# Copying the full attention's scores out of PSUM with VectorE, and giving the freed bank to the other attentions

## The reference, cut to what matters

```python
scores = softmax(einsum('bhqd,bhkd->bhqk', q, k) * scale)
entropy = -sum(scores * log(clip(scores, 1e-8)), axis=-1)
max_attn = scores.max(axis=-1)
influence = scores.sum(axis=-2)
importance = -entropy.mean(1)*0.4 + max_attn.mean(1)*0.3 + influence.mean(1)*0.3
_, idx = top_k(importance, 51)
```

## Time and profile before

| what | value |
|---|---|
| median of 3 runs | 1926.42 us (1925.96 to 1930.85) |
| the profiled execution | 1930.84 us, of it 1928.7 us from first to last instruction |
| mean granted TensorE clock | 0.692 of full speed |
| busy: PE, DVE, ACT, POOL | 1487.1, 1223.3, 1001.2, 389.4 us |
| first and last score matmul of the full attention | 229.5 and 1778.7 us |
| one batch's period in the middle of the run | 211.6 us for 64 slots |

### The profile page before, as it was taken

How to read it: one execution, slowest core, us unless ns; L and a number is a source line. 1 busy time by engine, 2 the same in 40 slices (tenths; PEclk the granted TensorE clock), 3 DMA queues, 4 the chain that set the end, 5 groups by cost and what they waited for, 6 DMA issues and landing times.

```text
span 1928.7 us, 25028 instructions
## 1 busy us (share of the span) xinstructions
PE 1487.1 (77%) x7949; PEld 652.0 (34%) x7949; DVE 1223.3 (63%) x3203; ACT 1001.2 (52%) x2478; POOL 389.4 (20%) x900
## 2 busy tenths in 40 slices
PE   1786797888788788788788878878878878678645
PEld 1333432343334333344234333334334322321312
DVE  1503556877787477856787478857786577787211
ACT  1051376457556555656556655565654657546122
POOL 3102301330133012310233023301221012110100
PEclk9566577659666777677766876677766867665555
DMA  2110210122012110122012111211011002200100
GB/s 59 31 47 11 57 34 17 42 50 41 6 50 52 23 23 14 45 46 45 14 39 52 28 19 36 53 26 33 14 34 36 12 14 45 27 13 12 17 8 5
DMA packets 65619, 59.17 MB, mean 31 GB/s; under 512 B 11936, under 2 KB 63184, under 8 KB 65488
## 3 DMA queue, kind: packets, MB, share of 16 engines
q1 hardware_dynamic: 65488, 57.58, 14.2%
HBM read 39.10 MB, written 18.27 MB: 30 GB/s over the span
## 4 chain that ended last, share of the span: by engine, by line
PE 50%; DVE 22%; ACT 15%; issue 7%; POOL 3%; DMA 2%; SPq 0%; ACTq 0%; POOLq 0%; DVEq 0%
PE bank L1276 8%; PE bank L1316 7%; DVE junk L978 5%; ACT setup L827 4%; PE bank L1268 4%; PE bank L1244 3%; PE bank L1221 3%; PE bank L1299 3%; DVE nm L946 3%; ACT pT L813 2%; DVE nmB L1068 2%; DVE nm L933 2%; PE bank L1259 2%; PE bank L1251 2%; PE bank L1200 2%
## 5 line engine op out<-in xcount | busy, mean ns | idle before, releaser
L827 ACT ACTIVATE setup<-bank,nmB 128x512 f32<-128x512 f32 x512 | 350.4, 684 | 340.7 <-DVE nmB L1068 339.5
L978 DVE SCALAR_TENSOR_TENSOR junk<-bank,thr,setup 128x512 f32<-128x512 f32 x512 | 379.2, 741 | 96.5 <-POOL thr L695 92.6
L1068 DVE TENSOR_REDUCE nmB<-bank 128x1 f32<-128x512 f32 x512 | 351.1, 686 | 111.5 <-PE bank L1268 111.3
L1268 PE MATMUL bank<-k_stacks,q_stacks 48*128 48x512 bf16 x512 | 254.5, 499 | 151.8 <-DVE junk L978 150.1
L695 POOL TENSOR_TENSOR thr<-lnZ,nmB 128x1 f32<-128x1 f32 x512 | 96.7, 190 | 1223.5 <-ACT lnZ L830 1223.2
L813 ACT ACTIVATE pT<-bank 128x512 f32<-128x512 f32 x320 | 174.3, 590 | 133.5 <-PE bank L1229 132.1
L1276 PE MATMUL bank<-setup,rz 128*1 128x512 f32 x1024 | 203.0, 879 | 0.0
L1268 PEld LDWEIGHTS bank<-k_stacks,q_stacks 48*128 48x128 bf16 x512 | 49.9, 98 | 384.2 <-DVE junk L978 285.3
L1221 PE MATMUL bank<-q_stacks,k_stacks 55*128 55x384 bf16 (+3 forms) x512 | 138.9, 346 | 36.6 <-ACT pT L813 30.7
L933 DVE TENSOR_REDUCE nm<-bank 128x4 f32<-128x512 f32 x128 | 86.5, 687 | 65.8 <-PE bank L1196 65.8
L909 ACT ACTIVATE p<-bank 115x512 f32<-115x512 f32 x128 | 75.1, 587 | 81.9 <-PE bank L1435 81.8
(11 more groups left out here) (195 smaller groups left out, 2327.9 us busy)
## 6 DMA issues: line engine op xcount, KB each, us to landing
part_dram<-part SPq DMA_DIRECT2D x16, 768.0 KB, 3.2
q_stacks<-part_dram SPq DMA_DIRECT2D x192, 64.0 KB
k_stacks<-part_dram SPq DMA_DIRECT2D x192, 64.0 KB
s_stacks<-part_dram SPq DMA_DIRECT2D x48, 128.0 KB
x<-in_L_attn_a_x_dram SPq DMA_DIRECT2D x8, 256.0 KB, 7.2
x_dram<-x SPq DMA_DIRECT2D x8, 256.0 KB, 2.2
x<-x_dram SPq DMA_DIRECT2D x8, 256.0 KB, 2.9
out_dram<-x SPq DMA_DIRECT2D x8, 256.0 KB, 2.2
```

The costliest lines, as they stand in the source:

```text
L827: act.activation(E[:, n % NE, :], RING[n % RN][:, :], ACT.Exp, bias=nmB[mb % 2][:, h, t:t + 1], accum_out=Z[mb % 2][:, h, t:t + 1]).then_i ...
L978: dve.scalar_tensor_tensor(out=junk[:, :], in0=RING[n % RN][:, :], scalar=thr[mb % 2][:, h, t:t + 1], in1=E[:, n % NE, :], op0=ALU.max, op ...
L1068: dve.tensor_reduce(nmB[mb % 2][:, h, t:t + 1], RING[n % RN][:, :], AX_X, ALU.max, negate=True).then_inc(s_bm, 1)
L1268: pe.matmul(RING[n % RN][:, :], qst[1][0:B_SC, h, t * P:(t + 1) * P], kst[1][0:B_SC, h, :], start=True, stop=True).then_inc(s_bs, 1)
```

## The change

- DVE no longer only takes the maximum of a tile of scores. One `tensor_scalar` multiplies the tile by -1, writes it to an SBUF buffer `negs` (four of them), and gives its row minimum, which is the negated maximum.
- ACT's exponential reads `negs` with scale -1; DVE's entropy step reads `negs` too, with signs turned (`min` for `max`), and POOL's subtraction is turned round.
- PE's ring has two banks (0 and 1) and is free when the copy has been made. `LEAD` is 2: PE writes tile n at the head of its slot n-2.
- The entropy step comes one slot later (`STT_LAG = 2`): tile n at the end of DVE's slot n+2.
- Bank 2 goes to the causal and the small attention: their first tiles and minus-max tiles take banks 3, 4 and 2 in turn.

```diff
+        NS = 4
+        negs = [sb(f"negs{i}", [P, T]) for i in range(NS)]
...
-        RING = (bank[0], bank[1], bank[2])
+        RING = (bank[0], bank[1])
+        TILE_BANK = (3, 4, 2)
...
-        LEAD = 1
+        LEAD = 2
+        STT_LAG = 2
...
-                use(3 + u % 2, z + A1_AT + u // 2, "a1", b, u)
+                use(TILE_BANK[u % 3], z + A1_AT + u // 2, "a1", b, u)
...
-                        act.activation(E[:, n % NE, :], RING[n % RN][:, :], ACT.Exp, bias=nmB[mb % 2][:, h, t:t + 1],
+                        act.activation(E[:, n % NE, :], negs[n % NS][:, :], ACT.Exp, scale=-1.0,
+                                       bias=nmB[mb % 2][:, h, t:t + 1],
...
-                    dve.scalar_tensor_tensor(out=junk[:, :], in0=RING[n % RN][:, :], scalar=thr[mb % 2][:, h, t:t + 1],
-                                             in1=E[:, n % NE, :], op0=ALU.max, op1=ALU.mult,
+                    dve.scalar_tensor_tensor(out=junk[:, :], in0=negs[n % NS][:, :], scalar=thr[mb % 2][:, h, t:t + 1],
+                                             in1=E[:, n % NE, :], op0=ALU.min, op1=ALU.mult,
...
-                        dve.tensor_reduce(nmB[mb % 2][:, h, t:t + 1], RING[n % RN][:, :], AX_X, ALU.max, negate=True
-                                          ).then_inc(s_bm, 1)
+                        if n >= NS:
+                            dve.wait_ge(s_be, n - NS + 1)
+
+                        dve.tensor_scalar(negs[n % NS][:, :], RING[n % RN][:, :], -1.0, None, ALU.mult, ALU.min,
+                                          accum_out=nmB[mb % 2][:, h, t:t + 1]).then_inc(s_bm, 1)
...
-                    if before:
-                        entropy(*before)
+                    lagging = main_tile(g - STT_LAG)
+                    if lagging:
+                        entropy(*lagging)
...
                     if n >= RN:
-                        pe.wait_ge(s_bn, n - RN + 1)
+                        pe.wait_ge(s_bm, n - RN + 1)
```

More of the change, by code:

```diff
@@ L197, in hybrid_block @@
         s_rows = sem("constant_rows_in_stacks")
-        s_full = {k: sem(f"bank{k}_uses_written") for k in (3, 4, 7)}
-        s_free = {k: sem(f"bank{k}_uses_read") for k in (3, 4, 5, 7)}
+        s_full = {k: sem(f"bank{k}_uses_written") for k in (2, 3, 4, 7)}
+        s_free = {k: sem(f"bank{k}_uses_read") for k in (2, 3, 4, 5, 7)}
         s_xin = sem("x_loaded")
@@ L256, in hybrid_block @@
         s_bs = sem("full_scores")
-        s_bm = sem("full_maxima")
+        s_bm = sem("full_scores_copied_with_maxima")
         s_be = sem("full_exponentials")
@@ L536, in hybrid_block @@
             for h in range(H):
[L537 removed]
+                use(TILE_BANK[h % 3], z + S1_AT + h // 2, "s1", b, h)
                 use(5, z + S2_AT + S_GANG * (h // HPQ) + h % HPQ, "s2", b, h)
@@ L549, in hybrid_block @@
                 use(7, z + DOWN[k], "down", k, b)
-        turn = {3: {}, 4: {}, 5: {}, 7: {}}
+        turn = {2: {}, 3: {}, 4: {}, 5: {}, 7: {}}
         for slot, k, name in sorted(uses, key=lambda e: e[0]):
@@ L603, in _ @@
                             if b:
-                                last = ("a2", b - 1, N2 // 2 * (f + 1) - 1)
-                                sp.wait_ge(s_full[4], turn[4][last] + 1)
+                                u = N2 // 2 * (f + 1) - 1
+                                k = TILE_BANK[u % 3]
+                                sp.wait_ge(s_full[k], turn[k]["a2", b - 1, u] + 1)
                             load_half(0, b, f, AL)
@@ L694, in _ @@
                         pool.wait_ge(s_bz, n + 1)
-                        pool.tensor_tensor(thr[mb % 2][:, h, t:t + 1], lnZ[mb % 2][:, h, t:t + 1],
-                                           nmB[mb % 2][:, h, t:t + 1], ALU.subtract).then_inc(s_bt, 1)
+                        pool.tensor_tensor(thr[mb % 2][:, h, t:t + 1], nmB[mb % 2][:, h, t:t + 1],
+                                           lnZ[mb % 2][:, h, t:t + 1], ALU.subtract).then_inc(s_bt, 1)
                     for b, a in own_slots(g):
@@ L811, in _ @@
                                     act.wait_ge(s_pv[0], 3 * (NG * b + gang - 1) + c + 1)
-                                act.wait_ge(s_full[3 + u % 2], turn[3 + u % 2]["a2", b, u] + 1)
+                                act.wait_ge(s_full[TILE_BANK[u % 3]], turn[TILE_BANK[u % 3]]["a2", b, u] + 1)
                                 act.activation(pT[:, js[0]:js[0] + len(js), c * T:c * T + WIDTH[c]],
-                                               bank[3 + u % 2][:, :].rearrange("p (j q) -> p j q", j=len(js)),
-                                               ACT.Exp).then_inc(s_free[3 + u % 2], 1)
+                                               bank[TILE_BANK[u % 3]][:, :].rearrange("p (j q) -> p j q", j=len(js)),
+                                               ACT.Exp).then_inc(s_free[TILE_BANK[u % 3]], 1)
                         for j in range(NG):
@@ L928, in causal_maxima @@
                 def causal_maxima(b, u):
-                    k, blocks = 3 + u % 2, FIRST_TILES[u % NF]
+                    k, blocks = TILE_BANK[u % 3], FIRST_TILES[u % NF]
                     h = 2 * (u // NF) + blocks[0][0]
@@ L943, in small_maxima @@
                 def small_maxima(b, h):
-                    k = 3 + h % 2
+                    k = TILE_BANK[h % 3]
                     dve.wait_ge(s_full[k], turn[k]["s1", b, h] + 1)
@@ L987, in own_importance @@
                     dve.wait_ge(s_imp, 4 * b + 1)
-                    dve.scalar_tensor_tensor(out=t2[:, :, :], in0=t1[:, :, :], scalar=LOG_CLIP, in1=thr[s][:, :, :],
+                    dve.scalar_tensor_tensor(out=t2[:, :, :], in0=t1[:, :, :], scalar=-LOG_CLIP, in1=thr[s][:, :, :],
                                              op0=ALU.add, op1=ALU.subtract).then_inc(s_imp, 1)
                     dve.wait_ge(s_imp, 4 * b + 2)
-                    dve.scalar_tensor_tensor(out=t3[:, :, :], in0=t2[:, :, :], scalar=0.4 / 0.3, in1=rz[s][:, :, :],
+                    dve.scalar_tensor_tensor(out=t3[:, :, :], in0=t2[:, :, :], scalar=-0.4 / 0.3, in1=rz[s][:, :, :],
                                              op0=ALU.mult, op1=ALU.add).then_inc(s_imp, 1)
@@ L1074, in _ @@
                         if a == A_TMAX - 1:
-                            dve.wait_ge(s_free[3], turn[3]["a1", b, N1 - 2] + 1)
-                            dve.wait_ge(s_free[4], turn[4]["a1", b, N1 - 1] + 1)
+                            for u in range(N1 - 3, N1):
+                                k = TILE_BANK[u % 3]
+                                dve.wait_ge(s_free[k], turn[k]["a1", b, u] + 1)
                             dve.tensor_tensor(nm[0][:, 1:NT, :], nm[0][:, 1:NT, :], nml[:, 1:NT, :], ALU.min
@@ L1181, in causal_scores @@
                 def causal_scores(b, u):
-                    k = 3 + u % 2
+                    k = TILE_BANK[u % 3]
                     claim(k, "a1", b, u)
@@ L1235, in weigh @@
                     g, c = w // 3, w % 3
-                    for u in (g * G2 + CHUNK_END[c] - 1, g * G2 + CHUNK_END[c]):
-                        pe.wait_ge(s_free[3 + u % 2], turn[3 + u % 2]["a2", b, u] + 1)
+                    for u in range(g * G2 + max(0, CHUNK_END[c] - 2), g * G2 + CHUNK_END[c] + 1):
+                        pe.wait_ge(s_free[TILE_BANK[u % 3]], turn[TILE_BANK[u % 3]]["a2", b, u] + 1)
                     if c == 0:
@@ L1427, in _ @@
                             claim(5, "tmax", b)
-                            pe.wait_ge(s_free[4], turn[4]["s1", b, H - 1] + 1)
+                            k = TILE_BANK[(H - 1) % 3]
+                            pe.wait_ge(s_free[k], turn[k]["s1", b, H - 1] + 1)
                             transpose_max(1, bank[5]).then_inc(s_mt, 1)
```

3 lines of the change are left out of this document (1 added, 2 removed).

## The result

The changed kernel takes 1999.76 us (median of 4 runs, 1994.43 to 2006.28) against 1928.63 for the kernel before in the same session (4 runs, 1925.96 to 1941.84). The ratio is 1.0347, 95% interval 1.0314 to 1.038: slower, by about 71 us, where the forecast was 42 more. The profiled execution took 2001.17 us, its span 1999.0.

What follows compares the result with a forecast made beforehand. No engine was full; PE and DVE went nearly in step, a slot costing about the longer one's work. Terms summed to +5.8 us a period, times 7.3 = +42 us on 1926.4: 1968 us, range 1895 to 2010.

Steps and rivals of the forecast that it cites:

- The release of the ring: PE's score-matmul head is released one DVE instruction later, by the copy: +7.5 us a period, bounds 2.7 to 9.5.
- 11 chains: Of PE's 14 head waits a period, 11 counted as separate slot chains, each paying the copy's 0.68 us.
- The copy for the maximum: DVE's copy with accumulator, 751 ns against 686 for the maximum: +1.4 us a period, between 0 and 4.2.
- The entropy step out of SBUF: DVE's entropy step with two SBUF inputs, 695 to 752 ns against today's 741: no change, 0.
- The rival of half rate: DVE's entropy step with two SBUF sources at half throughput, 1.28 us: about 2095 us in all; chance 0.03.
- DVE against GpSimd: Two-input entropy step contends with POOL: +1.5 us a period, between 0 and 4.4; rival with +4.4, 1989 us, chance 0.04.
- The exponential: ACT's exponential out of SBUF goes from 684 to some 724 ns, hidden by ACT's idle time: 0.
- The lag of the entropy step: Entropy step one slot later removes DVE's 10.5 us of threshold waits: -0.9 us a period, up to 4.
- Three tile banks: A third bank for first tiles shortens PE's waits for DVE and ACT: -3.7 us a period, from 0 to -8.
- the mechanism's own range: Whole-kernel time if the forecast's mechanism holds: 1940 to 2005 us, chance 0.63.
- PE's clock: PE's granted clock, 0.73 in the period, taken as unchanged; nothing in the sum follows it if it moves.
- The rival in which DVE gets ahead: DVE finishes whole slots early in PE's long slots, so the release costs nothing: about 1880 us; chance 0.20.

Runs made afterwards that it cites:

- before_gate: Kernel before with one added wait: the score matmul of tile n also waits for the maximum of tile n-1; 2011.98 us, ratio 1.0449.
- copy_only: Kernel before with the SBUF copy read by exponential and entropy step; ring of three, lead, lag and tile banks as before; 1972.1 us, 1.025.
- copy_act: Kernel before with the SBUF copy used by the exponential alone, the entropy step still reading PSUM; 1954.52 us, ratio 1.0126.
- stt_lag1: Changed kernel with the entropy step back at one slot's lag (STT_LAG 1 for 2); 2003.22 us, ratio 1.0361.
- lead1_lag1: Changed kernel with LEAD 1 for 2 and the entropy step at one slot's lag; 1913.29 us, ratio 0.9868.
- lead1: Changed kernel with LEAD 1 for 2, so PE's head waits for the copy of tile g-1; 1904.45 us, ratio 0.9878.
- ring3_lead1: Changed kernel with three ring banks, two banks for first tiles, and LEAD 1; 1910.83 us, ratio 0.9882.
- rz_lag: Changed kernel with DVE's inversion of the sums and the influence matmuls one slot later; 1993.09 us, ratio 1.0323.
- ring3: Changed kernel with bank 2 given back: three ring banks, two for first tiles, LEAD still 2; 1926.54 us, ratio 0.9997.
- copy_gate: Kernel before with the SBUF copy for exponential and entropy step, plus the added wait for the maximum of tile n-1; 2023.91 us, 1.0453.

## Why the prediction was right, step by step

**The release of the ring** is what makes the change slow, as forecast. It is shown from both sides: put in alone it costs 4.5%, taken out of the changed kernel (by LEAD, which also moves the score matmuls, or by the ring, which also takes the third tile bank away) it gives 3.4 to 4.5%. The term was 7.5 us a period. Alone, in before_gate, it is 6.9 in a middle period, but 66.7 us from the first score matmul to the last instead of 7.3 x 7.5 = 55: there the multiplication by 7.3 falls short, since the first and last batches pay more than a middle one. (For the whole change it holds: 7.3 x 10.45 = 76, measured 70.3.) Its wait is also a little dearer than the copy's: at the boundary at 999.64 us of before_gate the head starts 0.84 us after the maximum has started, where it started 0.75 after the copy. In the changed kernel the heads' waits grew by 11.7 a period (14 waits, now 18) and 79.2 over the run. 18 x 0.68 = 12.2 agrees with that better than my 11 chains: I had not counted the heads that came just in time before and wait now.

**The copy for the maximum**, +1.4, measures 0: 684 ns for 686. The nearest row by form (751) was the wrong one. The bound by size and source (684, the product out of PSUM in the earlier trace rows) was the price.

**The entropy step out of SBUF**, 0, was right: median 743, within 695 to 752. The rival of half rate, about 1.28 us, is refuted. The Trainium skill has this rule in the Vector Engine (DVE) Microarchitecture Reference, section "Points that are easy to get wrong"; the measured median, 743 ns, decides against it for this instruction.

**DVE against GpSimd**, +1.5 a period or 11 us, was too small: copy_only less copy_act is 24 us, near the bound of 4.4 a period that the rival took (32 us). But a sum per period was the wrong place for it: the middle periods of the two kernels are equal, and what contention costs shows in the first and last batches. I had priced only DVE's delay. The timeline of the kernel after shows both sides:

```profile
1059.68 2.18 POOL L678 TENSOR_TENSOR rest<-qf,part 128x512 f32<-128x512 f32 x1
...
1060.78 1.64 DVE L985 SCALAR_TENSOR_TENSOR junk<-negs,thr,setup 128x512 f32<-128x512 f32 x1
...
1062.04 0.42 POOL L701 TENSOR_TENSOR thr<-nmB,lnZ 128x1 f32<-128x1 f32 x1 [0.18 <-ACT lnZ L837]
...
1062.42 1.15 POOL L678 TENSOR_TENSOR rest<-qf,part 128x512 f32<-128x512 f32 x1
...
1062.96 1.16 DVE L985 SCALAR_TENSOR_TENSOR junk<-negs,thr,setup 128x512 f32<-128x512 f32 x1
...
1063.09 0.60 PE L1280 MATMUL bank<-k_stacks,q_stacks 48*128 48x512 bf16 x1 [2.13 <-DVE negs L1078]
```

The entropy step of 1060.78 takes 1.64 us beside POOL's 2.18, the next 1.16 beside POOL's 1.15, the threshold 0.42 instead of 0.19, and PE's head at 1063.09 had waited 2.13 us. The mean threshold went from 190 to 286 ns and the layer norm, on whose result PE's transposes wait, from 794 to 935. That a DVE instruction with two SBUF inputs contends with a GpSimd instruction that reads SBUF is in the Trainium skill, SBUF — State Buffer, section "Who interferes with whom"; the trace agrees (1.64 us beside POOL, for a median of 743 ns).

**The exponential**, 0, is 718 ns where some 724 was said. Whether it is free is open: copy_act has nothing else new than this and the copy, and it is 1.3% slower; of the 22.2 us between the spans 5.8 lie ahead of the first score matmul (235.3 for 229.5), where the two kernels are the same.

**The lag of the entropy step**, -0.9, measures 0 (stt_lag1, lead1_lag1). "What is late next" was answered wrongly: not the inputs of DVE's maxima, but the inversion of the sums, which the change left at slot g-1.

**Three tile banks**, -3.7 a period or -27 us. The waits in front of the first tiles did fall in the changed kernel: for DVE's maxima from 39.4 us to 9.3, for ACT from 30.7 to 24.9. Of the first the small attention's are 15.3 in the kernel before, 4.6 in before_gate and 1.1 in the changed kernel:

```profile
L1310 PE MATMUL bank<-kcst,s_stacks 48*128 48x115 bf16 x512 | 54.9, 253 | 16.5 <-DVE nm L946 15.3
```

```profile
L1311 PE MATMUL bank<-kcst,s_stacks 48*128 48x115 bf16 x512 | 54.0, 252 | 5.8 <-DVE nm L946 4.6
```

So in before_gate, with two tile banks, they fall too (in all to 22.1 for DVE and 21.2 for ACT): when PE is held at its head, the tiles' banks are free by the time it comes. So 17 of the 30 us are the other term seen again. Between lead1 and ring3_lead1 the bank is worth 20 us of waits, about 2.7 a period, and no time that could be separated from the other difference between them.

**The sum.** Every term was added; the costs do not add (2.5% and 4.5% make 4.5%). Heads and tile banks are two doors to the same queue: time lost at one is not lost at the other. A release too small outside the middle, too small a contention, and gains of lag and tile bank that mostly weren't there, left the forecast at +5.8 a period for +10.45. Of the 10.45 before_gate alone shows 6.9; which part of the change makes the other 3.5 no run says. The time still lies in the mechanism's own range of 1940 to 2005, near its upper end. The direction and the main term were right for the reason given. Without the terms that measured nothing or nearly nothing (+1.4, -0.9, -3.7) the same sum would have given +9.0 a period, 66 us, near the 71 measured; but part of that nearness is luck, since the 1.5 for contention in it is not found in a middle period and the release is larger at the ends of the run than in the middle.

**PE's clock** was set down as unchanged, with the remark that nothing in the sum followed it. It wasn't: 25.7 of the 70.3 us are PE's busy time. The rival in which DVE gets ahead did not come: waits at the heads rose. What it asked for came with LEAD = 1.

**Open.** What makes PE's busy time move. Over all these kernels the same 7949 matmuls take from 1429.4 us (lead1_lag1) to 1529.6 (copy_only), and more idle time doesn't mean a longer run: lead1 has 33.5 us more of it than before and is 20.9 us shorter. The idle share of the span doesn't order the clocks either: 23% goes with 0.676 (copy_act) and 0.692 (before), 24 to 25% with 0.669 (after) and 0.695 (lead1). No run was made that changes the clock alone. The nearest is the start of before and before_gate, where the same instructions at 0.74 and 0.51 of full speed bring the first score matmul at 229.5 and 241.6 us: there a lower clock goes with a later time and nothing in the program differs, but it is one pair of executions. For the rest of the run, whether the clock is a cause or a sign is not settled; nor is which of the copy and the longer exponential costs copy_act its 1.3%.

## What to carry to other kernels

Ask of a ring which instruction in the reader's in-order queue frees the bank at the moment when the writer wants it. More lead with fewer banks can move that instruction later, though each reader frees its bank sooner: here one slot of lead with two banks takes 4.5% less time than two slots. The version to keep is the changed kernel with LEAD = 1: well below the changed kernel, and 1.2% below the kernel before (0.9878 [0.9805, 0.9952]). Before a difference is put down to an edit, look at where the first instruction that the edit touches starts: here up to 12 us of a difference stood ahead of it. When one reader of a sum is lagged to get rid of a wait, look for the next reader that has kept its place (here lagging that one too only moved the wait on), and count an operand moved to SBUF on both engines that meet there.

## What the runs showed of the hardware that was not expected

- The same matmul at two speeds. The view of the score matmul (duration min/median/max) in lead1, and then in the kernel after:

```profile
L1280 PE MATMUL bank<-k_stacks,q_stacks x512: 373/387/631, 232.8 to 1758.4; 48*128 48x512 bf16 x171
```

```profile
L1280 PE MATMUL bank<-k_stacks,q_stacks x512: 375/602/631, 227.4 to 1846.5; 48*128 48x512 bf16 x171
```

The shortest and the longest are alike, some 374 and 631 ns, which I read as the two levels of the clock, 2.4 and 1.2 GHz, though no row gives the clock of a single matmul; the median is 387 in one kernel and 602 in the other. So a matmul's median says which level most of them met, and a longer PE busy time need not be more work.

- A `tensor_scalar` with an accumulator, PSUM to SBUF, 128x512 f32, takes 684 ns with the constant -1 as its scalar, and 751 in the ranking, whose scalar is a column of `imp` (L1018 of the kernel after). Which of their differences makes the 67 ns was not tried.
- The middle periods of ten kernels stand at five lengths: 208.2 us (lead1, lead1_lag1, ring3_lead1), 211.6 (before), 215.0 (copy_act, copy_only), 218.5 (before_gate), about 222 (after, rz_lag, stt_lag1). These lie in even steps of some 3.4 us, which over 7.3 periods is 25 us or 1.3%. Within one length PE's busy and idle time make up for each other: of 221.9 us PE is busy for 178.6 in rz_lag and 174.9 in stt_lag1. So quite different edits give the same length, a small edit may cost nothing or a whole step, and two costs need not add; prices of 1 to 2% read from these kernels, those above included, are no finer than that. ring3 and copy_gate repeat less evenly. The cause is open.
